# A four-layer graph network on one core: another order in the first layer, the fourth layer's source rows made in the third, loads moved up, and the first layer's softmax weights by three VectorE operations and two exponents

## The reference

```python
# layer 0: attention over the edges of a target, 4 heads
alpha = (q_s[dst] + k_s[src] + e_s) * inv_sqrt_c + gate * edge_weight
alpha = where(alpha >= 0, alpha, 0.2 * alpha)
ex = exp(alpha - segment_max(alpha, dst)[dst])
out = segment_sum(v[src] * (ex / (segment_sum(ex, dst)[dst] + 1e-16)), dst) + bias
# layer 1: mean of neighbours, two products
relu((concat([h, segment_mean(h[src], dst)]) @ W1 + b1) @ W2 + b2)
# layer 2: one of 8 matrices per edge
segment_sum((h @ weight[r])[src], dst), r = rel
# layer 3: per edge type relu(src @ W_e[t].T + b_e[t]), summed by target and type,
# concatenated with relu(h), then @ W_n[node_type].T + b_n, + h
x = layernorm(x + layer(x))      # after each of the four
```

## Time and profile before

| | |
|---|---|
| Median of 3 runs | 1717.78 us (1715.58 to 1718.99) |
| Profiled execution | 1722.77 us, span 1721.0 us |
| PE busy | 1390.8 us (81%) |
| DVE busy | 1410.1 us (82%) |
| ACT busy | 1120.2 us (65%) |
| POOL busy | 1230.3 us (71%) |
| Moved by DMA | 205.06 MB, 119 GB/s |

### The profile page before, as it was taken

One profiled execution on the slowest core, in us unless ns is written; L12 is line 12 of the kernel. 1 busy time (PEld: TensorE's weight loads), 2 busy tenths in 40 slices (PEclk: granted clock), 3 DMA queues, 4 the chain that ended last, 5 costly groups with the idle time before them and its releaser, 6 DMA issues.

```text
span 1721.0 us, 22842 instructions
## 1 busy us (share of the span) xinstructions
PE 1390.8 (81%) x6078; PEld 902.0 (52%) x6078; DVE 1410.1 (82%) x3005; ACT 1120.2 (65%) x2769; POOL 1230.3 (71%) x910
## 2 busy tenths in 40 slices
PE   4687777777777755787878589999998699999995
PEld 2454444544445434666666355555555355555552
DVE  4688888888888874998889679999998578877774
ACT  1567877778777783999999836666665344334442
POOL 7877777777788877778888387776330668888874
PEclk9678999999999987989999889999999899999998
DMA  7334444444434343677777535555543434333320
GB/s 169 85 68 101 112 98 98 105 104 112 99 98 108 82 130 73 187 201 192 197 196 194 161 87 144 150 141 137 148 119 94 99 94 101 99 94 93 98 74 22
DMA packets 165796, 205.06 MB, mean 119 GB/s; under 512 B 66825, under 2 KB 97920, under 8 KB 165668
## 3 DMA queue, kind: packets, MB, share of 16 engines
q1 hardware_dynamic: 108068, 179.45, 38.8%
q0 software_dynamic: 57600, 24.15, 8.0%
HBM read 147.12 MB, written 70.80 MB: 127 GB/s over the span
## 4 chain that ended last, share of the span: by engine, by line
PE 48%; DVE 16%; ACT 12%; issue 12%; POOL 9%; DMA 2%; SPq 1%; POOLq 0%; DVEq 0%; ACTq 0%
PE po L1323 22%; PE pt L1312 6%; POOL slot_all L528 6%; DVE masked L937 5%; DVE bst L732 4%; ACT x L1039 3%; PE pb L1329 2%; PE pb L1561 2%; PE po L1318 2%; PE po L1383 2%; PE pc L1431 2%; ACT so L1039 2%; PE pc L1312 2%; ACT do L1039 2%; ACT res L1039 1%
## 5 line engine op out<-in xcount | busy, mean ns | idle before, releaser
L528 POOL DMA_INDIRECT xs<-target_rows,slot_all x236 | 316.9, 1343 | 160.9 <-issue 68.8
L1039 ACT ACTIVATE x<-y,nmr,rst 125x128 f32<-125x128 f32 x800 | 322.3, 480 | 43.2 <-DVE nmr L757 43.2
L1323 PE MATMUL po<-wnt,rt 128*125 128x384 f32 x800 | 290.1, 508 | 0.0
L1312 PE MATMUL pt<-ident,x 125*128 125x125 f32 x800 | 134.6, 295 | 111.2 <-issue 82.3
L1323 PEld LDWEIGHTS po<-wnt,rt 128*125 128x125 f32 x800 | 158.3, 201 | 92.3 <-issue 14.4
L1323 PE MATMUL po<-wnt,run 128*125 128x384 f32 x600 | 201.5, 486 | 0.0
L535 POOL DMA_INDIRECT out_rows<-do,last_all x100 | 146.6, 1466 | 60.7 <-issue 40.0
L528 POOL DMA_INDIRECT xs<-in_x,src_all x100 | 133.8, 1338 | 53.7 <-issue 53.7
L1312 PEld LDWEIGHTS pt<-ident,x 125*128 125x128 f32 x800 | 100.1, 154 | 136.9 <-issue 100.9
L1039 ACT ACTIVATE do<-yd,nmr,rst 125x128 f32<-125x128 f32 x400 | 163.5, 482 | 6.2 <-DVE nmr L757 6.2
L1039 ACT ACTIVATE res<-sel,nmr,rst 125x128 f32<-125x128 f32 x400 | 163.5, 482 | 3.8 <-DVE nmr L757 2.6
(11 more groups left out here) (186 smaller groups left out, 3024.5 us busy)
## 6 DMA issues: line engine op xcount, KB each, us to landing
xin<-in_x SPq DMA_DIRECT2D x100, 224.0 KB
out_rows<-res SPq DMA_DIRECT2D x100, 224.0 KB
same<-same_d SPq DMA_DIRECT2D x75, 250.0 KB, 4.1
source_rows<-so SPq DMA_DIRECT2D x75, 224.0 KB
target_rows<-do SPq DMA_DIRECT2D x75, 224.0 KB
xs<-source_rows SPq DMA_DIRECT2D x59, 224.0 KB
rel<-in_etype SPq DMA_DIRECT2D x50, 250.0 KB, 4.8
xd<-target_rows SPq DMA_DIRECT2D x46, 224.0 KB
```

The lines of the kernel that those rows point to most:

```text
L528: return nc.gpsimd.indirect_dma_start(out=to, out_offset=None, in_=table, in_offset=bass.IndirectOffsetOnAxis(ap=index, axis=0), bounds_ch ...
L1039: last = A(to[:, j, :], y[:, j, :], ACT.Identity, scale=rst[s][:, k:k + 1], bias=nmr[s][:, k:k + 1])
L1312: last = nc.tensor.transpose(tile_of(to, j), rows_[:, j, :], ident[0:R, 0:R])
L1323: last = mm(po[0:R, j * 512:j * 512 + NT * D], left(j), wnt[:, k, :, :].rearrange("k t d -> k (t d)"), start=start, stop=stop, skip_group_ ...
```

## The change

- First layer, scan: the running value is now kept as max(value + start, score), with start 0 or a large negative number at a target's first edge, and `start_d` loses its extra element. VectorE then makes both exponents' arguments (one addition, two subtractions, one subtraction before); ScalarE only takes the two exponents.
- First layer, order: GpSimd gathers source rows and target rows of a chunk in two calls with separate semaphores, the sources before the slot work; 5 marks an iteration instead of 6, and 52 slots (`SOONER` 13) before the second layer instead of 76. ScalarE makes the first four result rows before the denominators and evacuates the next sources before the second block's rows. TensorE turns the next sources and does the features' product before the first dense products.
- The fourth layer's source rows: in the second layer ScalarE no longer makes them. VectorE keeps a factor per row (`factors1` into `again_all`), and in the third layer ScalarE multiplies the loaded third-layer source rows by it (`source_rows2`) and SyncE stores them (`store_sources2`).
- SyncE: the first loads of the third and fourth layer are issued inside the last iteration of the layer before (`aux` and a new buffer `rel3` serve the fourth), and the last stores of the first layer come after the second layer's first loads. Node types are gathered later.

```diff
@@ SyncE @@
+            rows1(2)
+            targets1(1)
+            store_sources0(EC - 1)
             store_targets0(EC - 2)
-            rows1(2)
             store_targets0(EC - 1)
-            targets1(1)
...
-                for part in PARTS:
-                    sp.dma_start(rows(s_rows[2])[c][part, :], flat(so3[b])[part, :]).then_inc(q["stS"][b], 16)
...
             def sources2(c):
                 k, q, o = c % 3, ph[2], ph[1]
                 sp.wait_ge(q["tS"], at(c - 2))
+                sp.wait_ge(q["nS"], at(c - 2))
...
+            def store_sources2(c):
+                b, q = c % 2, ph[2]
+                sp.wait_ge(q["nS"], c + 1)
+                for part in PARTS:
+                    sp.dma_start(rows(s_rows[2])[c][part, :], flat(so3[b])[part, :]).then_inc(q["stS"][b], 16)
...
+                if c == EC - 1:
+                    sources2(0)
+                    relations2(0)
+                    sources2(1)
+                    relations2(1)
+                    sums2(0)
+                    targets2(0)
+                    sums2(1)
+                    sources2(2)
...
             stored(1)
+            store_sources2(0)
             sources2(3)
+            store_sources2(1)
...
                 if there(c + 2):
                     sums2(c + 2)
+                if c == EC - 1:
+                    sources3(0)
+                    targets3(0)
+                    sums3(0)
+                    sources3(1)
+                    sums3(1)
+                    sources3(2)
                 if c >= 1:
                     store2(c - 1)
+                if there(c + 2):
+                    store_sources2(c + 2)
                 store_dense(d - 7)
@@ GpSimd @@
             for c in range(EC):
                 q = ph[0]
+                if there(c + 3):
+                    pool.wait_ge(q["yb"], c + 1)
+                    pool.wait_ge(q["tS"], c + 1)
+                    sources0(c + 3)
                 if c < MARKED:
                     marks0(MARKS * c, MARKS * (c + 1))
...
                 if there(c + 3):
-                    pool.wait_ge(q["yb"], c + 1)
                     pool.wait_ge(q["tD"], c + 1)
                     pool.wait_ge(q["nF"], c + 1)
-                    rows0(c + 3)
+                    targets0(c + 3)
...
-                late = SOONER + c // 3
-                if c % 3 == 0 and there(late):
-                    slots1(late * T, (late + 1) * T, s_slot[1 + c // 3])
-                else:
-                    types2(typed, typed + 3)
-                    typed += 3
+                late = SOONER + 2 * (c // 3) + c % 3
+                if c % 3 < 2 and there(late):
+                    k, n = slot_ring(late)
+                    pool.wait_ge(s_slot[k], 16 * T * (n - 1))
+                    slots1(late * T, (late + 1) * T, s_slot[k])
+                elif c > EC // 2:
+                    types2(typed, typed + 2)
+                    typed += 2
+            types2(typed, typed + 2 * T)
@@ VectorE @@
-                step(scan(run, 0, score, aux[b][:, :], ALU.max, ALU.add))
-                V.tensor_tensor(wb, run[:, 0, 0:C], score, ALU.subtract).then_inc(q["vE"], 1)
+                step(scan(run, 0, aux[b][:, :], score, ALU.add, ALU.max))
+                step(V.tensor_tensor(wb, run[:, 0, 0:C], aux[b][:, :], ALU.add))
+                V.tensor_tensor(wa, score, run[:, 0, 1:C + 1], ALU.subtract)
+                V.tensor_tensor(wb, wb, run[:, 0, 1:C + 1], ALU.subtract).then_inc(q["vE"], 1)
...
+            def factors1(c, s, third, first):
+
+                of = lambda a, g: a[s][:, g * T:(g + 1) * T]
+                step(V.scalar_tensor_tensor(out=of(tmp, 0), in0=of(ve, first), scalar=1.0 / D, in1=of(rst, first), op0=ALU.mult, op1=ALU.mult))
+                V.tensor_tensor(again_all[:, c, :], of(tmp, 0), of(rst, third), ALU.mult).then_inc(ph[1]["vF"], 1)
@@ ScalarE @@
-                A(wa, wb, ACT.Relu)
-                A(wb, wb, ACT.Relu, scale=-1.0).then_inc(q["eR"], 1)
-                act.wait_ge(q["eR"], c + 1)
-                A(wb, wb, ACT.Exp, scale=-1.0)
-                A(wa, wa, ACT.Exp, scale=-1.0).then_inc(q["eX"], 1)
+                A(wb, wb, ACT.Exp)
+                A(wa, wa, ACT.Exp).then_inc(q["eX"], 1)
...
                 rows_of(2 * c, s, (4, 0))
+                if there(c + 1):
+                    results_of(2 * c, s, 2)
                 sums0(c)
-                if c < EC - 1:
-                    evacuate_dense(2 * c)
+                if there(c + 1):
+                    evacuate_rt(2 * c)
+                    evacuate_xt(2 * c)
                     weights0(c + 1)
+                if there(c + 2):
+                    evacuate_sources(c + 2, 0, 0)
                 rows_of(2 * c + 1, s, (5, 1))
...
-                normalize(so[b], ys[b], k % 2, 4)
-                normalize(so3[b], ys[b], k % 2, 1).then_inc(q["nS"], 1)
+                normalize(so[b], ys[b], k % 2, 4).then_inc(q["nS"], 1)
...
+            def source_rows2(c):
+                b, q = c % 2, ph[2]
+                act.wait_ge(q["stS"][b], (c // 2) * ROWS)
+                for j in range(T):
+                    last = A(so3[b][:, j, :], xs2[c % 3][:, j, :], ACT.Identity, scale=again_all[:, c, j:j + 1], bias=none[:, 0:1])
+                last.then_inc(q["nS"], 1)
...
                     evacuate_sources(c + 3, 2, 7)
                 evacuate_xt(d - 1)
+                if there(c + 2):
+                    source_rows2(c + 2)
                 act.wait_ge(q["stD"][b], (c // 2) * ROWS)
                 normalize(do[b], yd[b], k % 2, 3).then_inc(q["nD"], 1)
@@ TensorE @@
                     turn_xt(2 * c)
-                    dense_products(2 * c)
-                    turn_rt(2 * c + 1)
                     if there(c + 2):
                         score_features(c + 2)
                         turn_sources0(c + 2)
+                    dense_products(2 * c)
+                    if there(c + 2):
                         pe.wait_ge(ph[0]["eS"], c + 3)
+                    turn_rt(2 * c + 1)
+                    if there(c + 2):
+                        score_sources(c + 2)
                     turn_xt(2 * c + 1)
                     if there(c + 2):
-                        score_sources(c + 2)
                         turn_targets0(c + 2)
```

More of the change, by code:

```diff
@@ L134, in gnn_kernel @@
         aux = two(sb, "aux", [D, C])
[L135 removed]
+        rel, rel3 = two(sb, "rel", [D, C], I32), two(sb, "rel3_", [D, C], I32)
         run, run2 = sb("run", [D, 3, C + 1]), sb("run2", [D, 3, C + 1])
@@ L138, in gnn_kernel @@
         den = sb("den", [R, T * H])
+        again_all, none = sb("again_all", [R, EC, T]), sb("none", [R, 1])
         headsel = sb("headsel", [D, H])
@@ L182, in gnn_kernel @@
                **{k: [sem(f"layer{n}_{k}_{i}") for i in range(ring)] for k, ring in RINGS[n].items()}} for n in range(4)]
-        s_slot = [sem(f"layer1_slots_{i}") for i in range(EC - SOONER + 1)]
+        s_slot = [sem(f"layer1_slots_{i}") for i in range(1 + 3)]
         s_types = sem("s_types")
@@ L376, in _ @@
             stored(0)
-            for c in range(EC):
-                d = block_of(1, c)
-                load_dense(d + 3)
-                if there(c + 3):
-                    rows1(c + 3)
-                if there(c + 2):
-                    targets1(c + 2)
-                    sums1(c + 2)
-                if c >= 1:
-                    store_sources1(c - 1)
-                    store_targets1(c - 1)
-                    store_dense(d - 7)
             def sources2(c):
@@ L481, in sums3 @@
                 if c < 2:
-                    sp.wait_ge(ph[2]["vA"], EC - c)
-                    sp.wait_ge(ph[2]["vM"], (EC - c) * (REL - 1))
-                sp.dma_start(same[b][:, :], to_all(same_d, c)).then_inc(q["sm"][b], 16)
-                sp.dma_start(rel[b][:, :], to_all(etype3, c)).then_inc(q["sm"][b], 16)
-            sources3(0)
-            targets3(0)
-            sums3(0)
-            sources3(1)
+                    sp.wait_ge(ph[1]["vA"], EC)
+                sp.dma_start(aux[b][:, :], to_all(same_d, c)).then_inc(q["sm"][b], 16)
+                sp.dma_start(rel3[b][:, :], to_all(etype3, c)).then_inc(q["sm"][b], 16)
+            for c in range(EC):
+                d = block_of(2, c)
+                if d + 3 < NC:
+                    load_dense(d + 3)
+                if there(c + 4):
+                    sources2(c + 4)
+                if there(c + 2):
+                    relations2(c + 2)
+                if there(c + 1):
+                    targets2(c + 1)
+                if there(c + 2):
+                    sums2(c + 2)
+                if c == EC - 1:
[5 more added lines that the diff above has]
+                    sources3(2)
+                if c >= 1:
+                    store2(c - 1)
+                if there(c + 2):
+                    store_sources2(c + 2)
+                store_dense(d - 7)
             targets3(1)
-            sums3(1)
-            sources3(2)
```

(27 more changed lines are left out.)

124 lines of the change are left out of this document (49 added, 75 removed), and 2 rows, old and new, of the table RINGS.

## The result

| | before | after |
|---|---|---|
| Median | 1718.38 us (1715.58 to 1720.11, 4 runs) | 1841.71 us (1840.34 to 1843.89, 4 runs) |
| Profiled execution, its span | 1722.77, 1721.0 us | 1840.35, 1838.6 us |

The ratio is 1.0721, with a 95% interval from 1.0701 to 1.074: slower by 123 us. 1841 was forecast.

The account below looks back on a forecast made before the run. It took engine loops, ScalarE, then VectorE as the first three layers' bounds; 53 us gained and 176 lost gave +123 on 1722.8, 1845.8, and a median 5 us below, 1841 us; range 1770 to 1885.

Parts of the forecast that it names:

- Third layer, forecast 176 lost: SyncE's new store waits, relation numbers come late for the masks; loop 21.2 us instead of 13.0, 22 times: 176 us lost.
- landing: Third layer, relation numbers from issue to arrival: 4.9 us, between 4.4 and 5.7, taken from a measured row.
- Now SyncE's iteration c ends with a store that waits: Third layer: the store waits for count c+3 of the new rows; relation numbers behind it leave 12 us later.
- The clock, forecast as 2.1 us: Third layer: idle TensorE returns at about half speed; 0, 1.4 or 2.8 us more a turn, 2.1 taken.
- The rival in which the clock holds: Third layer: loop closes but TensorE keeps full clock, 19.1 us a period, 130 lost, 1795 us; chance 0.12.
- Faster rival, 1668: Third layer: new rows' count is reached before SyncE's wait, costing some 3 us; 1668 us, chance 0.1.
- First layer, forecast 26: VectorE becomes the bound at 22.6 us an iteration instead of 23.9; 1.3 us over 20 iterations, 26 us gained.
- Both cut the loop: First layer: ScalarE's dropped rectifications and filled wait, and TensorE's earlier source-row turn, each shorten the loop through the engines.
- First joint, forecast 12: Between first and second layers: GpSimd has 8 fewer gathers behind its last wait on VectorE; 12 us gained, bounds 8 and 16.
- Second layer, forecast 9: ScalarE loses one normalisation, VectorE becomes the bound at 11.6 instead of 12.0 us; 24 periods, 9 us gained.
- third joint: Before the fourth layer: last target rows leave sooner, ScalarE's dense work becomes the bound; 4.5 us gained (0 to 6).
- that rival: Whole kernel: loop as forecast, first layer stays at 23.9, slow clock costs its full 2.8 us; 1884 us, chance 0.1.

Follow-up runs that it names:

- the versions that mend the queue: Changed kernel with the relation numbers issued ahead of the waiting store: 1663.4 us; or with that store an iteration later and source rows' load behind it: 1665.81 us.

## Why the prediction was right, point by point

- **Third layer, forecast 176 lost, measured 181.7.** The mechanism was right: the count comes in the wrong iteration, one queue, relation numbers late. Terms, forecast and read in one turn: issues 3.4 and 3.37, landing 4.9 and 5.16, masks and scales 1.9 and 1.99, scan to evacuation 6.3 + 2.1 and 7.85 (9.28 in the turn behind it, 8.4 in the mean), new rows 2.6 and 2.61. The landing, read up to the first use, was 0.3 us too short. By the Trainium skill (DMA: Bandwidth & Descriptors, Anatomy of one DMA), whose fit is given for transfers that GpSimd issues, it would be an estimated 2.6 us; this load is issued by SyncE and the trace has twice that, so the measured row was the one to take.
- **The step that was incomplete:** "Now SyncE's iteration c ends with a store that waits". The source rows' load has the same wait right behind it. For the forecast that changed nothing; for a repair it decides: moving the store alone brings 72 of 182 us.
- **The clock, forecast as 2.1 us.** It took 1.5 in this turn and 3.0 in the next, and 2.1 in the mean of thirteen. 56 transposes that leave no long idle time bring 1.00 and periods of 19.5 us in the mean, near the 19.1 of the sum at full clock. The rival in which the clock holds (1795) is out by the granted 0.81, where the kernel before had 1.00.
- **Faster rival, 1668:** the count is not reached early, but the versions that mend the queue run at 1663.4 and 1665.8. The price of that rival was right within 5 us, its third layer too (3 forecast, 2.1 measured).
- **First layer, forecast 26, measured 33.7.** Two errors, which pull opposite ways. The steady iteration is 23.04 us and not 22.6, though VectorE is the bound as forecast, busy 456.2 of 475.7 us or 22.1 of 23.04: it does not close its last gaps. And the early iterations, which I left out, give 17.9 of the 32 us between the first and the last scores (the first seven periods take 158.2 us before and 140.3 after). The old weights or the old order alone leave them at 149.3 and 149.0, so each carries about 9 of it. The step "Both cut the loop" is half wrong: with the old weights the new order leaves the period at 23.90. That the two rectifications are what keeps it there is read from VectorE's wait of 2.30 us for the roots; no run takes them out alone. ScalarE's wait ahead of the denominators, which I had taken as filled, is still 1.4 us in the mean.
- **First joint, forecast 12, measured 9.7.** The bound is GpSimd as said, and the wait fell from 18.27 to 8.08 us. GpSimd's first row gather starts at 612.25 in place of 657.17 us, 11.2 more than the layer's 33.7: the count of 8 issues was a good price. The rows are then turned 9.4 us after it and not 7.8, so 9.7 shows. What the count leaves out is GpSimd's own lag: undone alone, its plan costs 19 us, since the shorter iterations have no idle time left for more gathers. The cover for it that the prediction named, 1 us under VectorE, was that near.
- **Second layer, forecast 9, measured 12.7; drain 1.5 and 3.4; third joint 4.5 and 4.6.** VectorE is the bound at 11.48 (11.6 forecast). The old period was 12.0, as the prediction took it. The two factors' price was right: two operations of 0.20 and 0.16 us. At the third joint the bound was named rightly too: ScalarE's dense rows, and no longer the gathered ones. The loads moved up, and that joint with them, have no run of their own.
- **The sum, forecast 123 lost, measured 117.6 between the two traces.** The gains were 64.1 us and not 53, the loss 181.7 and not 176, so the forecast for the profiled execution, 1845.8, was 5.4 too long against 1840.35. The prediction then took the median 5 us below that execution, as before the change; after it the median lies 1.4 above. That 1841 meets the median of 1841.71 within 1 us is therefore partly luck: two errors of some 5 us cancel.
- **A slip in a rival.** With the slow clock at its full 2.8 us the loss is 176 + 22 x 0.7 = 191 us and not 193, and that rival 1882 and not 1884. Nothing else hangs on it.

## What to carry to other kernels

Before a wait is put into a queue that issues loads, write down which iteration's work makes its count, what stands behind it, and which of those loads has the least slack: here one load with only 6.3 us of slack stood behind it, and the layer became 182 us longer, and issuing that one load ahead of the wait turned +123 us into -57. Look for every place where the change asks for the same count; mending the first only moves the stall to the next. When one engine is freed, ask at once what a queue that was hidden under it will do at the next joint.

## What the runs showed of the hardware that I had not expected

- TensorE came back slow behind idle times of about 3 us that recur in turns of 21 us. In the run with 32 transposes, of fourteen turns with 2.3 to 3.8 us idle ahead of the sums' four transposes, these took 1.2 us in eight (behind 2.99 us idle, for one), 0.70 in two (behind 2.98 and 3.21) and something between in four. In the run with 56 transposes and at most 1.03 us idle they took 0.70 in all fifteen. Before the run I had taken such a remainder for harmless. The idle time by itself does not tell which turn is slow.
- The same load of 250 KB was in use 5.17 us after its issue in the median of 19 turns (4.77 to 5.75), with four transfers of a quarter megabyte just ahead of it in the queue, and 4.6 us in the median of 18 (4.30 to 5.18) with the source rows alone.
